# Moving one GpSimd instruction per head pair in a fused FFN, attention and FFN kernel: the keys' low part before the key sum

## What is computed

```python
x = x + 0.5 * ffn(layernorm(x))      # 2 shared experts, 8 routed ones, top 2, with a capacity
x = x + attention(layernorm(x))      # 16 heads of 64
x = x + 0.5 * ffn(layernorm(x))
```

```python
qkv = x @ w_qkv.T
q, k, v = to_heads(q), to_heads(k), to_heads(v)
q = q * cos + rotate_half(q) * sin + fenc
k = k * cos + rotate_half(k) * sin + fenc
dots = jnp.einsum('bhid,bhjd->bhij', q, k) * scale
attn = jax.nn.softmax(dots, axis=-1)
out = jnp.einsum('bhij,bhjd->bhid', attn, v)
out = out.transpose(0, 2, 1, 3).reshape(b, n, INNER)
return out @ w_out.T + b_out
```

## Time and profile before

| | us |
|---|---|
| median of 3 runs | 1249.49 (1247.38 to 1252.7) |
| the profiled execution | 1255.02 |
| its span, first to last instruction | 1253.2 |
| TensorE busy | 1220.5 (97%) |
| VectorE busy | 949.9 (76%) |
| GpSimd busy | 907.9 (72%) |
| ScalarE busy | 618.5 (49%) |
| granted TensorE clock, mean | 0.997 |

### The profile page before, as it was taken

How to read it: one execution, slowest core, us unless ns; L and a number is a source line. 1 busy time by engine, 2 the same in 40 slices (tenths; PEclk the granted TensorE clock), 3 DMA queues, 4 the chain that set the end, 5 groups by cost and what they waited for, 6 DMA issues and landing times.

```text
span 1253.2 us, 22010 instructions
## 1 busy us (share of the span) xinstructions
PE 1220.5 (97%) x8242; PEld 849.0 (68%) x8242; DVE 949.9 (76%) x1439; ACT 618.5 (49%) x905; POOL 907.9 (72%) x652
## 2 busy tenths in 40 slices
PE   5999999899999999999999999999999999999998
PEld 4788888556656566666656565666656556788887
DVE  6666787788988888888878888788878866466642
ACT  4443422465555546555555545555655554333422
POOL 0543446898998898898999899899989862543444
PEclk9999999999999999999999999999999999899999
DMA  5442141133323233232323233233323221442240
GB/s 172 136 186 74 63 137 33 38 65 57 73 52 69 61 64 65 61 70 52 78 53 77 53 68 62 56 74 59 71 53 73 56 44 20 143 145 71 83 161 17
DMA packets 118681, 95.41 MB, mean 76 GB/s; under 512 B 75760, under 2 KB 85008, under 8 KB 118320
## 3 DMA queue, kind: packets, MB, share of 16 engines
q1 hardware_dynamic: 118064, 93.75, 30.5%
q10 hardware_dynamic: 512, 0.26, 0.1%
HBM read 57.53 MB, written 2.88 MB: 48 GB/s over the span
## 4 chain that ended last, share of the span: by engine, by line
PE 80%; POOL 9%; issue 5%; DVE 3%; ACT 2%; DMA 1%; SPq 0%; POOLq 0%; DVEq 0%; ACTq 0%
PE banks L460 16%; PE banks L1160 15%; PE banks L1137 12%; PE banks L474 11%; PE banks L1069 5%; PE banks L988 5%; PE banks L1177 4%; PE banks L1142 4%; PE banks L1187 3%; POOL work L1439 3%; PE banks L996 3%; POOL turn L1429 2%; POOL qk_l L1434 1%; POOL turn L1423 1%; POOL o_t L1446 1%
## 5 line engine op out<-in xcount | busy, mean ns | idle before, releaser
L1000 DVE TENSOR_REDUCE neg_max<-banks 128x2 f32<-128x1024 f32 x256 | 301.6, 1225 | 14.4 <-PE banks L988 10.3
L1267 ACT ACTIVATE work<-banks 128x1024 f32<-128x1024 f32 x256 | 262.3, 1026 | 89.7 <-PE banks L1142 66.0
L1160 PE MATMUL banks<-work 128*64 128x512 f32 x1024 | 233.8, 598 | 0.0
L1439 POOL TENSOR_TENSOR work<-work 128x1024 f32<-128x1024 f32 x64 | 160.3, 2505 | 60.5 <-PE banks L1160 60.5
L1429 POOL TENSOR_TENSOR turn<-turn,side_turned 128x512 f32<-128x512 f32 x128 | 174.0, 1379 | 31.4 <-DMA side_turned<-side 30.9
L1423 POOL TENSOR_TENSOR turn<-turn,fenc 128x512 f32<-128x512 f32 x128 | 162.8, 1291 | 2.4 <-DVE side L1338 2.4
L1434 POOL TENSOR_TENSOR qk_l<-turn,qk_h 128x512 fp32r<-128x512 f32 x128 | 162.9, 1293 | 0.4 <-ACT qk_h L977 0.4
L1160 PEld LDWEIGHTS banks<-work 128*64 128x64 f32 x1024 | 67.8, 136 | 132.6 <-issue 130.1
L1359 DVE TENSOR_TENSOR work<-work 128x1024 f32<-128x1024 f32 x64 | 104.1, 1626 | 33.3 <-PE banks L1160 33.2
L977 ACT ACTIVATE qk_h<-turn 128x512 fp32r<-128x512 f32 x128 | 80.6, 631 | 95.7 <-POOL turn L1429 95.5
L792 POOL TENSOR_TENSOR work<-work 128x512 f32<-128x512 f32 x44 | 56.5, 1290 | 98.0 <-DVE work L710 58.9
(11 more groups left out here) (175 smaller groups left out, 2544.6 us busy)
## 6 DMA issues: line engine op xcount, KB each, us to landing
work<-share SPq DMA_DIRECT2D x32, 1024.0 KB, 9.4
side_turned<-side SPq DMA_DIRECT2D x256, 128.0 KB, 3.1
rec_all<-rec_d SPq DMA_DIRECT2D x128, 128.0 KB, 2.9
x_tok<-in_x SPq DMA_DIRECT2D x8, 256.0 KB, 6.2
out<-x_tok SPq DMA_DIRECT2D x8, 256.0 KB, 9.7
work<-in_w_gate_up SPq DMA_DIRECT2D x1, 1280.0 KB, 7.2
work<-in_w_qk SPq DMA_DIRECT2D x1, 1024.0 KB, 12.6
den_d<-den_rows ACTq DMA_DIRECT2D x64, 4.0 KB
```

What stands on the lines that cost most here:

```text
L1000: return nc.vector.tensor_reduce(neg_max[:, g % 2, qt::DH], of, AX.X, ALU.max, negate=True)
L1160: ins = nc.tensor.matmul(o_bank(g)[OWN[h], :], v_all[:, kt, n * DH:(n + 1) * DH], pt[:, g % 2, kt, h * T:(h + 1) * T], start=(kt == 0), st ...
L1267: nc.scalar.activation(pt[:, g % 2, kt, :], S[kt].rearrange("p h q -> p (h q)"), ACT.Exp, scale=QSCALE).then_inc(s["probs"], 1)
L1439: nc.gpsimd.tensor_tensor(pt[:, g % 2, 2, :], pt[:, g % 2, 2, :], pt[:, g % 2, 3, :], ALU.add).then_inc(s["second_sum"], 1)
```

## The change

In GpSimd's period, the low part of the keys is made before `second_sum`, and the low part of the queries stays behind it:

```diff
                     if exists(ahead):
                         turned_part(ahead, K, s["k_sum"], 1)
                         turned_part(ahead, Q, s["q_sum"], 2)
+                    if exists(ahead):
+                        low(ahead, K, s["k_high"])
                     if exists(p - 1):
                         second_sum(p - 1)
                     if exists(ahead):
-                        low(ahead, K, s["k_high"])
                         low(ahead, Q, s["q_high"]).then_inc(s["low"], 1)
                     if exists(new):
                         fourier_part(new, K, s["roped"], 1)
```

## The result

The changed kernel took **1276.62 us** (median of 5 runs, 1275.47 to 1278.76) against 1250.45 for the kernel before on the same chip: a ratio of 1.021, 95% interval 1.0195 to 1.0225, that is 26 us slower. The forecast was 1273.5 with a range of 1261 to 1292. The profiled execution has a span of 1277.0 us. In a later measurement it took 1278.1 against 1250.5 (1.0225, 1.0208 to 1.0242).

The account below looks back on a forecast made before the run. TensorE, busy 97% of the span, was taken as the bound; ordinary and late waits, half given back, made 26.7 us, less 3.3 existing, plus 0.6: +24 on 1249.5, so 1273.5 us, range 1261 to 1292.

Parts of the forecast that it names:

- The bound and the place: Attention stage goes at TensorE's pace; its waits at the denominators for GpSimd's key sum rise from 3.3 to 25 us or more.
- The price of the meeting: Low part of the keys beside VectorE's key sum: between 0 and 1.0 us, the upper end taken.
- the first rival: Low part and VectorE's sum run together in GpSimd's gap, so not slower: 1246 to 1251, or up to 1256; chance 9%.
- An ordinary period: Three things in line before the denominators: a new wait of about 0.75 us, 0.37 on average after giving back; 47 periods.
- Late periods: 13 periods whose turned parts end late, behind VectorE's sum: 1.4 us each at the denominators, half of it given back.
- The giving back: Swapped halves' DMA is issued at its old time despite TensorE's wait, so the next wait shrinks; half the loss returns.
- The sum: (47 x 0.75 + 13 x 1.4) / 2 = 26.7 us, minus 3.3 of existing waits: +23.4, with +0.6 for small effects +24.
- The third rival: VectorE's key sum is pushed behind GpSimd's, some 2 us each time, at one in six periods 20 us: 1293; chance 11%.

Follow-up runs that it names:

- the tied run: Changed order, with SyncE issuing the DMAs of the swapped halves only after that period's denominators: 1314.01 us (1.0515); the order before with the same wait took 1255.93.
- the two half runs: The changed order in every other period, the order before in the rest: odd periods 1278.78 us (1.0229), even periods 1269.48 us (1.0165).
- the odd run: The changed order in the odd periods alone, the order before in the even ones: 1278.78 us (1.0229).

## Why the prediction was right

- **The bound and the place.** TensorE's waits at the denominators for L1439 were to rise to 25 us or more in 35 or more times; they are 27.4 in 38. L1434's mean was to reach 1600 to 1800 ns; it is 1596. L1429's was to stay or fall: 1328 after 1379. One item was wrong: GpSimd's idle time before its key sum was to fall under 15 us and is 26.3, since in the periods behind a wait everything on GpSimd is early and it waits for the last value product. And the periods don't simply alternate between 12.7 and 13.4 us, as told above.
- **The price of the meeting.** Taken at the upper one of two ends, by the nearest row. It could have been read: the prediction says that no row shows the low part's price, but the trace before has one, while VectorE's sum of the earlier trace rows at 347.74 stands until 351.24:

```profile
350.12 2.26 POOL L1434 TENSOR_TENSOR qk_l<-turn,qk_h 128x512 fp32r<-128x512 f32 x1
```

That is 1.0 us over its plain 1.28. The runs without VectorE's sum confirm this price, and with it the rule of the Trainium skill, SBUF — State Buffer, section "Who interferes with whom": the trace agrees that a VectorE sum with both inputs in SBUF and a GpSimd instruction that reads SBUF exclude each other. One number beside it was a slip: the first rival's margin of 0.17 us is 633.81 - 633.49 = 0.32, with the 0.15 already in it.
- **An ordinary period** was put at 0.75 us. The one at 302.49 has an idle time of 0.59 us and is 0.67 us longer than 12.67, and many others have 0.50 and 0.58. The low part with VectorE's sum ahead of it takes 2.24 us from start to start, where I had added 1.25 + 1.08 = 2.33. Late periods, with a long turned pair, were put at 13 with 1.4 us; in the steady part five are left, with 1.15 to 1.39.
- **The giving back** was the step that fixed the size, read from one pair of rows. Its mechanism holds: the counts above, the tied run and the two half runs show it. Its size was put too high. Half comes back where all periods wait alike (both low parts ahead of the key sum). In the change it is less, because some issues of the DMAs take longer, and because GpSimd is not free early in the seven bias periods: the prediction's line 639.4 before 639.84 doesn't hold there, the turned parts start 6.04 us or more after the last denominators, though in five of the seven a wait came before, and six of these periods wait 0.54 to 0.75 us (the seventh holds the event at 560 us).
- **The sum.** From the denominators of the second group to those of the 60th there are 58 periods, which undisturbed take 51 x 12.67 + 7 x 13.12 = 738.0 us (the seven with a batch's first transposes are the longer ones). The changed kernel took 31.2 us more than that. Of these, 4.8 are the event at 560 us, and 26.4 are what the sum put at 26.7. The kernel before took 5.3 more: 2.0 for its own event at 347 us, and 3.3 elsewhere, by chance the same figure as the waits of the earlier trace rows, which lie in part outside these periods. So outside the events the change cost 23.1 us for a forecast of 23.4, and the events add 2.8. That the sum fits so closely is partly luck. From the tied run, 60.8 us more than undisturbed, less 58 x 0.28 for the tie itself, the full price without giving back comes to about 44.5 us (an estimate), where the prediction has 47 x 0.75 + 13 x 1.4 = 53.5; and of the 44.5 about 59% arrives, where the prediction has half. The two errors offset each other.
- **The third rival** was given its own 11% and left out of the forecast. In truth an event of its kind is part of the usual course: once before (at 347 us), once in each of the two profiles of the changed kernel (6.64 us at 560.61 and 3.37 us at 538.48, with 4.8 and 3.1 us for the two periods), two in the odd run. In these few profiles an event costs more behind the change than before it; whether it comes more often can't be told from them.

## What to carry to other kernels

An idle gap in front of an instruction on GpSimd isn't free for filling when a VectorE instruction with two SBUF inputs runs in it: look in the other engine's timeline for a recorded duration that is longer than its plain one. Add up what must pass in line before the consumer's need, both engines' parts in one sum. And ask what a wait doesn't delay: here a DMA that was issued at its old time gave some 40% of the loss back, and for the same reason half of the edits cost 20 or 29 us where all of them cost 26.

## What the runs showed of the hardware that I had not expected

- A VectorE instruction that waits for GpSimd usually gets in between two GpSimd instructions that follow one another, but not always. In the odd run a layer norm step on 128x8 elements stood for 6.11 us, until GpSimd had no more to do, and the key sum for 7.32 in another period:

```profile
772.22 6.11 DVE L293 SCALAR_TENSOR_TENSOR rs<-nt 128x8 f32<-128x8 f32 x1
...
986.02 7.32 DVE L1359 TENSOR_TENSOR work<-work 128x1024 f32<-128x1024 f32 x1 [0.93 <-PE banks L1160]
```

In the second profile of the changed kernel the longest wait was behind one instruction of GpSimd (3.37 us in all), so being shut out through four of them doesn't happen in every execution. What decides which of the two gets the turn stays open; no run here was made for it.

- Such an event costs more than its own wait. VectorE's products with the angles come late as well, so the next DMAs are issued at 570.14, 2.79 us after the start of the denominators, and the next denominators wait 0.91 us more. Besides, in the changed kernel's profile TensorE had been idle for 1.83 us before 567.35, and then its granted clock fell; windows of that stretch (us, busy time of each engine, clock third from the end):

```profile
560.00:567.00 7.00, 5.52 (x30) 3.26 (x26) 6.39 (x1) 2.46 (x4) 6.17 (x5) 1.00 0.14 38
567.00:569.00 2.00, 1.65 (x20) 1.07 (x22) 2.00 (x4) 0.39 (x1) 0.00 (x0) 0.94 0.00 0
569.00:571.00 2.00, 1.68 (x10) 0.86 (x7) 2.00 (x3) 0.43 (x1) 0.81 (x1) 0.50 0.01 2
571.00:575.00 4.00, 4.00 (x30) 3.17 (x30) 3.84 (x4) 2.56 (x3) 2.97 (x3) 0.85 0.65 138
```

The clock of 0.50 is the lower level, 1.2 GHz, for some 3.4 us (2 us at 0.50, and parts of the 2 us before them and the 4 behind). At half the clock that loses at most 1.7 us of the 4.8 (an estimate). Pairs of score products took 0.64 us there (at 569.04, for 0.39 to 0.40 at the full clock). The ordinary waits of 0.6 us do not show in the clock, whose mean over the whole execution is 0.999.
